# ScalarE's one-hot copies ahead of the first root in the opening of the window attention

## The reference

```python
h = token_mixer(x)
h = h + taylor_attention(layernorm(h), Wq, Wk, Wv, Wo)
h = h + expert_ffn_top2(layernorm(h), ...)             # 8 experts
h = h + relative_attention(layernorm(h), wq, wk, wv, wproj, bproj, rk_v, rk_h, rv_v, rv_h)
h = h + expert_ffn_top1(layernorm(h), Ws, bs, W1, b1, W2, b2)
```

```python
def _layernorm(x, eps=1e-05):
    return (x - mean(x)) / sqrt(var(x) + eps)

# 12 heads of 64, N = 750 tokens; token 0 stands apart, 749 lie on a grid 27 wide
q, k, v = (x @ w).reshape(B, N, 12, 64) for w in (wq, wk, wv)
attn = q @ k.T * scale + (q . rel_pos_embed(N, rk_v, rk_h)) * scale
attn = softmax(attn)
out  = attn @ v + (attn . rel_pos_embed(N, rv_v, rv_h))
return out @ wproj + bproj
```

## Time and profile before

| | |
|---|---|
| median of 3 runs | 1672.21 us (1671.56 to 1675.51) |
| the profiled execution | 1672.95 us, span 1671.2 us, mean granted clock 0.986 |
| TensorE busy | 1579.9 us, 95% |
| VectorE busy | 1179.5 us, 71% |
| ScalarE busy | 983.8 us, 59% |
| GpSimd busy | 388.5 us, 23% |
| the opening of the attention, 349 to 422 us | TensorE 60.73 us, ScalarE 37.40 us, clock 0.88 |
| its four batches, 422 to 1441 us | TensorE 993.29 us, clock 1.00 |

### The profile page before, as it was taken

One profiled execution on the slowest core, in us unless ns is written; L12 is line 12 of the kernel. 1 busy time (PEld: TensorE's weight loads), 2 busy tenths in 40 slices (PEclk: granted clock), 3 DMA queues, 4 the chain that ended last, 5 costly groups with the idle time before them and its releaser, 6 DMA issues. The chain is left out here.

```text
span 1671.2 us, 31054 instructions
## 1 busy us (share of the span) xinstructions
PE 1579.9 (95%) x11573; PEld 1465.1 (88%) x11573; DVE 1179.5 (71%) x2223; ACT 983.8 (59%) x1775; POOL 388.5 (23%) x421
## 2 busy tenths in 40 slices
PE   5999999978999999999999999999999999989997
PEld 5889999977899898889888889888899989878996
DVE  4887555548776786786786776777677688576554
ACT  5542222226678578678677668767767857462331
POOL 4132565540003002110210210310300310013442
PEclk9999999998999999999999999999999999899999
DMA  9212122264101101101100110110010111091221
GB/s 273 72 45 88 54 62 60 62 151 115 46 11 40 46 11 39 46 11 25 60 12 11 30 47 20 30 46 20 30 46 11 40 50 38 20 299 56 65 61 29
DMA packets 61951, 95.10 MB, mean 57 GB/s; under 512 B 15645, under 2 KB 46512, under 8 KB 61423
## 3 DMA queue, kind: packets, MB, share of 16 engines
q1 hardware_dynamic: 52606, 72.92, 15.0%
q0 software_dynamic: 9200, 20.21, 4.1%
HBM read 72.58 MB, written 21.06 MB: 56 GB/s over the span
## 5 line engine op out<-in xcount | busy, mean ns | idle before, releaser
L2761 DVE TENSOR_REDUCE a_nmx<-a_M 125x1 f32<-125x752 f32 x256 | 240.8, 940 | 125.8 <-PE a_M L2229 125.2
L2583 ACT ACTIVATE a_Phi<-a_S 125x756 fp32r<-125x756 f32 x288 | 231.0, 802 | 159.4 <-PE a_O L2352 146.5
L2886 DVE TENSOR_TENSOR a_Plo<-a_PT,a_Phi 125x756 fp32r<-125x756 f32 x288 | 281.2, 976 | 50.8 <-ACT a_PT L2583 50.0
L2583 ACT ACTIVATE a_PT<-a_S 125x756 f32<-125x756 f32 x288 | 229.9, 798 | 0.0
L1979 POOL TENSOR_TENSOR a_qlo<-a_work,a_qhi 127x750 fp32r<-127x750 f32 x48 | 79.3, 1660 | 566.1 <-PE a_S L2333 494.3
L2333 PE MATMUL a_S<-a_qhi,a_khi 128*125 128x378 f32 x576 | 154.8, 350 | 10.1 <-issue 7.1
L2345 PE MATMUL a_O<-a_Phi,a_vhi 125*128 125x378 f32 x576 | 150.3, 342 | 1.3 <-ACT a_PT L2583 1.3
L2352 PE MATMUL a_O<-a_Plo,a_vhi 125*128 125x378 f32 x576 | 147.4, 337 | 1.0 <-DVE a_Plo L2886 0.9
L2333 PE MATMUL a_S<-a_qlo,a_khi 128*125 128x378 f32 x576 | 147.0, 336 | 0.0
L2333 PE MATMUL a_S<-a_qhi,a_klo 128*125 128x378 f32 x576 | 146.9, 336 | 0.0
L2348 PE MATMUL a_O<-a_Phi,a_vlo 125*64 125x378 f32 x576 | 146.3, 335 | 0.0
(11 more groups left out here) (457 smaller groups left out, 3190.7 us busy)
## 6 DMA issues: line engine op xcount, KB each, us to landing
a_qhi<-a_rdens SPq DMA_DIRECT2D x48, 187.5 KB, 3.3
a_wkv<-a_w4k SPq DMA_DIRECT2D x8, 768.0 KB, 5.3
a_wq<-a_w4q SPq DMA_DIRECT2D x8, 768.0 KB, 6.7
a_wkv<-a_w4v SPq DMA_DIRECT2D x8, 768.0 KB, 5.8
m_w<-in_m_w SPq DMA_DIRECT2D x8, 576.0 KB, 9.0
m_X<-m_xn SPq DMA_DIRECT2D x8, 504.0 KB
m_w<-in_m_w SPq DMA_DIRECT2D x8, 384.0 KB, 5.5
m_w_ahead<-in_m_w SPq DMA_DIRECT2D x8, 384.0 KB, 7.1
```

The lines of the kernel that those rows point to most:

```text
L2583: last = nc.scalar.activation(to[:, wd % 2, :].rearrange("p (a l) -> p a l", a=2), psS[wd % 2][0:P, :, 0:HP], ACT.Exp, scale=SCALE)
L2761: v.tensor_reduce(nmx[:, u % 2, c:c + 1], bank[0:P, :, 0:376], AX.XY, ALU.max, negate=True).then_inc(sg["max_ready"], 1)
L2886: v.tensor_tensor(Plo[:, wd % 2, :], PT[:, wd % 2, :], Phi[:, wd % 2, :].bitcast(F32), ALU.subtract).then_inc(sg["exp_rest"], 1)
```

## The change

The wait for the variance and the root, which were the first two statements of ScalarE's stream, now stand behind the wait for the two tables and the six copies. Nothing else is changed.

```diff
         @block.scalar
         def _(act):
-            act.wait_ge(s_ln, 1)
-            nc.scalar.activation(rstd[:, 0:CH], rstd[:, 0:CH], ACT.Sqrt).then_inc(s_sd, 1)
             act.wait_ge(s_oh, 32)
             for hh in range(HG):
                 nc.scalar.activation(khi[64:128, hh, :], oh, ACT.Copy)
+            act.wait_ge(s_ln, 1)
+            nc.scalar.activation(rstd[:, 0:CH], rstd[:, 0:CH], ACT.Sqrt).then_inc(s_sd, 1)
```

## The result

| | before | changed |
|---|---|---|
| median of 22 runs each | 1671.35 us | 1674.33 us |
| lowest and highest | 1669.04, 1675.51 | 1672.25, 1678.83 |
| ratio, 95% interval | | 1.0019 (1.0011 to 1.0026) |
| a second set, 28 and 10 runs | 1673.23 us | 1677.41 us, ratio 1.0023 (1.0013 to 1.0032) |

The change costs 3.0 us by the medians, 3.2 by the first ratio (0.0019 x 1671) and 3.8 by the second. The forecast was 2.9 us, and 1675.2 us for the time; the measured 1674.33 lies lower mostly because the median of the kernel before came out at 1671.35 over 22 runs and not at the 1672.21 of its first three.

What follows compares the result with a forecast made beforehand. The late root delays TensorE's transposes, with idle products as the bound: 1.85 us at the full clock, 2.9 with the clock's fall, passed whole. On the median of 1672.21 that is 1675.1, given as 1675.2; range 1670.8 to just over 1679.1.

Steps and rivals of the forecast that it cites:

- Landing of the tables: ScalarE's wait for both tables' DMAs, now ahead of the root, was to end at 362.8 us.
- The two estimates that agreed: Tables' landing, by time of issue 363.0 us and backwards from the keys' weights 362.7 us.
- The forward one: Tables' landing counted forwards from `Plo`: 375 KB together, 1.7 us, so 360.5 us.
- Copies and load: On ScalarE after the landing, six copies of 4.41 us and the table load of 1.28 us precede the root.
- the rival that it gave: Table load with the page's drain: 4.3 us slower, 1676.5 us; one of several cases with chance 0.20 together.
- The root 3.2 us late: ScalarE's root ends at 368.76 instead of 365.58; VectorE's reciprocal and everything behind it come 3.2 us later.
- The clock: TensorE's hole of 3.5 us likely makes the clock fall; idle products end at 374.95 instead of 373.9 us.
- Second transposes: On TensorE, bound by the idle products, 1.85 us late at the full clock, 2.9 us with the clock's fall.
- rival 2: TensorE's hole appears but the clock does not fall: 1.85 us slower, 1674.1 us; chance 0.17.
- The delay passes whole: Nothing behind the second transposes swallows the delay; all 2.9 us reach the end.
- rival 1: Tables land by 359.6, copies and load fit ScalarE's idling, 1.33 us won: 1670.9 us; chance 0.10.
- Rival 4: Something swallows the delay or a later low-clock stretch shifts, 2 us or so; time stays at 1672; chance 0.08.

Runs made afterwards that it cites:

- second pair: Second profiles of the kernel before and of the changed kernel, both rerun unchanged; ratios to the kernel before 1.0003 and 1.0023.
- first pair of profiles: First profiles of the kernel before and of the changed kernel, nothing further altered; the changed kernel's ratio to the kernel before 1.0019.
- both remedies: Changed kernel with the table loaded first by a root of one number and a separate semaphore for the second table; ratio to the kernel before 1.0003.

## Why the prediction was right, and where it was not

- *Landing of the tables.* The open step. Forecast 362.8, which is 4.1 us from T; measured 363.75, 4.14 from T. The two estimates that agreed were right. The forward one, 360.5, is 1.8 from T and was 2.4 us short; even the first table alone (1.09 from T in the kernel that waits for it) landed no more than 0.7 us ahead of it.
- *Copies and load.* 4.41 and 1.28 us, back to back, the root 0.02 us behind the load. The drain of about 1380 ns that the Trainium skill has in "ScalarE: Activation LUTs", "What ACT_TABLE_LOAD costs", shows in none of the four profiles looked at: the instructions beside the load start and end within 0.02 us of it. The measurement decides, and the rival that it gave falls.
- *The root 3.2 us late.* 3.21 by the first transposes. The hole was to be 3.5 and was 3.17.
- *The clock.* It fell as forecast and rose again 3.4 us later. The 28 records: 4.35 us in the forecast (370.6 to 374.95), 4.73 measured. In all three profiles with a hole above 3 us at this place (3.17, 3.23 and 3.36) the clock fell; with the hole filled, or of 1.65 or 0.94 us, it did not.
- *Second transposes.* Forecast +2.9, measured +3.33 and +3.22. At the full clock the sum gives 10.75 + 4.27 = 15.02, which is 1.7 late (1.85 in the forecast, rival 2); the clock's share is the other 1.6 (1.05 in the forecast). The error lies in that term: the forecast let the clock be low from work's return to 3.56 us after it. It fell 0.9 us after the return and rose 4.3 after it (370.36, 371.3 and 374.7), so more of the idle products ran at the low clock: of the 1.6 us the 28 records cost 1.44 and the slower transposes 0.18.
- *The delay passes whole.* Right for a delay: 3.1 us at the last exponential in the second pair, 1.7 in the first, whose kernel before had the low stretch from 383.
- *The agreement at the end.* That 2.9 meets the medians' 3.0 so closely is in part luck: the sum was 0.3 to 0.4 us short at the second transposes, and the low stretch near 411, which the sum did not have and the changed kernel's profiles lack, gives 0.4 back.
- *A gain passes whole.* Not in general. The forecast did not rest on it, but rival 1 did (1670.9). "No transfer that arrives at a time of its own is waited for behind this point" holds for later and not always for earlier. Batch 1's outputs land shortly ahead of their use: two of the kernels whose second transposes come 1.34 and 1.50 us earlier wait for them and keep 0.76 and 0.74, while the third, with both remedies, keeps 1.42 of 1.50. The row of L2649 at 375.55 shows no idle time and nothing of how little was to spare. The kernel with both remedies is what rival 1 describes: its last exponential came 1.2 us early, in the fastest execution of its set, and the times of the set show no difference (1.0003, interval from 0.9994; rival 1 needs 0.9992).
- *Rival 4* was at work in the first pair of profiles, where the clock's low stretches hid 1.6 of the 2.8 us at the first exponential, and in the second pair the missing stretch near 411 took 0.4 of the 3.2. What part such stretches have in the medians is not shown.

## What to carry to other kernels

An instruction that was hidden because it stood ahead of a wait (here the table load) counts in full when its function is moved behind another wait; list what the compiler places before the moved instruction as well. A semaphore that two DMAs share delays the first one's user to the second one's landing: here by 3.05 us. When idle products are tuned to bridge a gap, a delay ahead of them is paid in full, and an advance beyond them is lost (with six products for 14 the changed kernel's second transposes followed the first after 4.03 us instead of 5.89); and before a gain is counted as passing on, look for the next DMA's slack, which a row without a wait doesn't show and which differs from one execution to the next.

## What I had not expected of the hardware

- Two tables of 187.5 KB each, issued 0.52 us apart on one queue, landed 3.05 us apart (1.09 and 4.14 us from T, in the kernel that waits for the first alone and in the changed one), with the DMA engines' share at 1.06 to 1.08 from 352 to 365. In the five profiles that show the first landing it is 0.97 to 1.29 us from T, in the five that show the second 3.66 to 4.15.
- A hole of 3.17 and one of 3.23 us on TensorE were followed by a fall of the clock to its 1.2 GHz level within 1 us of work's return (transposes of 0.33 us growing to 0.45); holes of 1.65 and 0.94 us at the same place were not. Ahead of the first scores the hole is 2.26 or 2.27 us in all four profiles of the two kernels; it was followed by a low stretch in both of the kernel before and in neither of the changed one.
- One kernel's low stretches differ from run to run: the clock from T to T + 64 us was 0.92 in one profile of the kernel before and 0.97 in the other, 1.7 us of time at the first exponential.
